# A two-layer graph convolution whose merges read 5 of 8 chunks, with the routing of finished nodes woven into the second layer's sums

## The reference

```python
xn = layernorm(x)                       # x: 3125 nodes x 256
# graph convolution, twice: 50000 edges (src, dst), sorted by dst, and a loop at every node
deg  = segment_sum(1, dst);  norm = rsqrt(deg)[src] * rsqrt(deg)[dst]
conv = lambda h, W, b: segment_sum((h @ W)[src] * norm, dst) + b
gnn  = conv(relu(conv(xn, W1, b1)), W2, b2)          # 256 -> 128 -> 256
# linear attention over all nodes (4 heads of 32, 4 memory slots), rmsnorm before and after
mix  = rmsnorm(attention(rmsnorm(xn)) @ w_out + b_out) + xn
x = x + gnn + mix
# mixture of experts: 8 experts, the best 2 of a token, hidden width 256
t = layernorm(x)
x = x + t + sum_e weight(t, e) * (gelu(t @ w1[e] + b1[e]) @ w2[e] + b2[e])
```

## Time and profile before

| | us |
|---|---|
| median of 3 runs | 755.34 |
| lowest and highest | 754.62, 762.78 |
| span of the profiled execution, first to last instruction | 754.8 |
| PE busy in it | 585.7 (78%) |
| DVE busy | 509.7 (68%) |
| ACT busy | 347.6 (46%) |
| POOL busy | 132.2 (18%) |

### The profile page before, as it was taken

The page is one execution under the profiler, slowest core; times in us unless marked ns, Lnnn a source line. Parts: engine busy times, 40 slices in busy tenths (PEclk is TensorE's granted clock), DMA queues, the critical chain, the costliest instruction groups (busy, mean ns, idle before and its releaser), DMA issues.

```text
span 754.8 us, 13942 instructions
## 1 busy us (share of the span) xinstructions
PE 585.7 (78%) x5198; PEld 516.7 (68%) x5198; DVE 509.7 (68%) x1114; ACT 347.6 (46%) x623; POOL 132.2 (18%) x133
## 2 busy tenths in 40 slices
PE   0889791879999999999599999989640499999500
PEld 0245351769999999987499999888530399999500
DVE  6773998459999999818556531299850577887534
ACT  0034773397777777710211111224240388999400
POOL 2000000000000000000000000018886145565600
PEclk9978996799999999999799999999755599999955
DMA  7999999301355531000056867503332245555198
GB/s 186 253 283 284 284 283 313 145 1 54 166 218 219 218 163 58 2 1 1 1 218 271 337 265 297 200 4 84 92 90 76 82 130 138 163 147 151 36 229 280
DMA packets 80158, 121.17 MB, mean 161 GB/s; under 512 B 8573, under 2 KB 68770, under 8 KB 78429
## 3 DMA queue, kind: packets, MB, share of 16 engines
q1 hardware_dynamic: 70621, 107.03, 46.8%
q0 software_dynamic: 9472, 13.27, 5.7%
HBM read 50.00 MB, written 72.21 MB: 162 GB/s over the span
## 4 chain that ended last, share of the span: by engine, by line
PE 48%; DVE 21%; DMA 9%; POOL 8%; issue 6%; ACT 5%; SPq 1%; DVEq 0%; ACTq 0%; POOLq 0%
PE psB L1216 21%; POOL expert_slots L571 8%; DVE hot L683 7%; PE psC L1122 3%; DMA back<-expert_out 3%; PE psC L1216 3%; PE psB L1369 3%; PE psA L1134 3%; DMA xs<-expert_slots 3%; PE psD L1134 2%; DMA acc<-in_x_dram 2%; PE psA L1357 2%; PE psC L1383 1%; ACT counts L1414 1%; PE psD L1383 1%
## 5 line engine op out<-in xcount | busy, mean ns | idle before, releaser
L1216 PE MATMUL psB<-hs,counts 125*128 125x256 f16 x1600 | 210.3, 275 | 3.3 <-DVE hs L790 2.7
L1216 PEld LDWEIGHTS psB<-hs,counts 125*128 125x128 f16 x1600 | 173.0, 140 | 4.9 <-issue 2.8
L683 DVE TENSOR_TENSOR hot<-iota_j,places 128x2048 bf16<-128x2048 bf16 x128 | 154.9, 1223 | 18.0 <-PE psA L1134 12.0
L563 POOL IOTA row_of<- 128x25 f32 x1 | 0.2, 238 | 475.3 <-PE psC L1216 475.3
L578 POOL DMA_INDIRECT expert_out<-y,to_row x64 | 65.8, 1029 | 62.3 <-DVE y L1060 49.4
L1414 ACT CAST counts<-psA 128x1000 f16<-128x1000 f32 x64 | 63.3, 989 | 15.2 <-PE psA L1134 15.2
L571 POOL DMA_INDIRECT expert_slots<-rows,place x50 | 62.1, 1241 | 45.2 <-issue 44.9
L1414 ACT CAST counts<-psD 128x1000 f16<-128x1000 f32 x64 | 63.6, 994 | 12.6 <-PE psD L1134 12.6
L1134 PE MATMUL psA<-hot 128*128 128x125 bf16 x512 | 49.4, 220 | 12.9 <-DVE hot L683 7.1
L1134 PEld LDWEIGHTS psA<-hot 128*128 128x128 bf16 x512 | 38.1, 98 | 22.8 <-DVE hot L683 12.4
L848 DVE TENSOR_TENSOR sum_both<-psB,sum_both 128x256 f32<-128x256 f32 x32 | 13.5, 422 | 57.7 <-ACT sum_both L1474 57.7
(11 more groups left out here) (286 smaller groups left out, 1067.0 us busy)
## 6 DMA issues: line engine op xcount, KB each, us to landing
expert_slots<-zeros SPq DMA_DIRECT2D x8, 3536.0 KB, 29.9
kept_counts<-counts SPq DMA_DIRECT2D x6, 4000.0 KB, 11.4
counts<-kept_counts SPq DMA_DIRECT2D x6, 4000.0 KB, 13.0
xs<-expert_slots SPq DMA_DIRECT2D x32, 272.0 KB, 3.1
back<-expert_out SPq DMA_DIRECT2D x5, 1120.0 KB
w_raw<-in_L_ffn_w_dram SPq DMA_DIRECT2D x2, 2048.0 KB, 11.5
acc<-in_x_dram SPq DMA_DIRECT2D x1, 2800.0 KB
out_dram<-acc SPq DMA_DIRECT2D x5, 560.0 KB
```

The lines of the kernel that those rows point to most:

```text
L683: v.tensor_tensor(hot[:, slot].rearrange("p g w n s -> p (g w) n s"), iota_j[:, :, :].unsqueeze(1).to_broadcast([P, 2 * pairs, P, PAIR]), ...
L1216: m = pe.matmul(sum_bank(g, d), counts5[0:PT, buf, a, d, :], hs2[0:PT, a, :, :].rearrange("p q f -> p (q f)"), start=a == 0 and first, sto ...
```

## The change

**Merges.** A window w of block c has steps between 125c + t and 125c + 124 + t, so a block's steps can lie in at most 5 chunks once all steps are moved up by 3 places (`AHEAD`): chunks 0 to 4, 1 to 5, 1 to 5, 2 to 6, 3 to 7 for blocks 0 to 4 (`chunks_of`). `merge` has 20 matmuls in place of 32, `merge_transposed` 2 + 10 for a node in place of 2 + 16.

**Layer 1** builds and sums chunks 7 down to 0. Before the sums of the eighth chunk in that order, blocks 4 and 3 are merged, in the middle of them blocks 2 and 1, after them block 0. The scale for layer 2 is now made in the beginning, together with that of layer 1, from a bound (the largest input plus the largest bias), so `spread_scale(1)`, the running maximum and its reductions are gone, and a block can be split into its halves as soon as it is there.

**Layer 2** sums chunks 1, 0, 2, 3, 4, 5, 6, 7; the first of them takes the blocks of features in the order 4 to 0. Block 0 is merged and routed inside chunk 5's sums, blocks 1 and 2 inside chunk 6's, block 3 inside chunk 7's and block 4 after them. The pieces of routing are written out by hand between fifths of a chunk (25 matmuls) on PE, and between the groups of sums on DVE and ACT.

**Memory.** `rows` and `tokT` get room of their own outside `counts`; `hs` and `sel` make place for `w1_now`, `xs`; the second weights `w2` lie in one tensor with the first (`w_split`); the outputs of `times_w2` move from psB and psC to psA and psD.

```diff
+FIRST_ORDER = [*range(CH - 1, -1, -1)]
+SECOND_ORDER = [1, 0, *range(BUFFERS, CH)]
+BLOCK_ORDER = [*range(C - 1, -1, -1)]
+AHEAD = 3
+def chunks_of(c):
+    first, last = AHEAD + PT * c, AHEAD + PT * c + PT - 1 + EDGE_TILES - 1
+    return [*range(first // P, last // P + 1)]
...
-                    for k in range(CH):
+                    for k in chunks_of(c):
                         for part in range(2):
...
-                    for k in range(CH):
...
-                    pe.wait_ge(sums_low_ok, SG * CH)
-                    for c in range(C):
-                        merge(c, max(c, 1), (psD, psA)[c % 2])
-                else:
-                    spread_scale(layer)
+            pe.wait_ge(counts_ok, UNITS * CH)
+            merge(0)
+            merge(1)
+            for i in range(2 * SLOTS):
+                add_sum((CH - 1) % BUFFERS, SUM_LIST, i, CH - 1)
+            merge(2)
+            merge(3)
+            for i in range(2 * SLOTS, len(SUM_LIST)):
+                add_sum((CH - 1) % BUFFERS, SUM_LIST, i, CH - 1)
+            merge(4)
...
-                        st.did(v.tensor_reduce(hs_max[0:PT, bass.ds(c + 1, 1)], hs[0:PT, bass.ds(W * c, W), :].rearrange("p d f -> p (d f)"),
-                                               AX.X, ALU.max))
-                    st.wait()
-                    make_scale(1)
...
-                if c >= 2:
-                    pe.wait_ge(token_full_ok, 3 * (c - 1))
+                    pe.wait_ge(token_full_ok, 3 * c)
...
+            second_sums(7, 0, Q)
+            ranks(1)
+            merge_transposed(3)
+            second_sums(7, Q, 2 * Q)
+            token_transposes(2)
+            second_sums(7, 2 * Q, 3 * Q)
+            logits(2)
+            times_w2(3)
+            second_sums(7, 3 * Q, 4 * Q)
+            ranks(2)
+            second_sums(7, 4 * Q, 5 * Q)
+            token_transposes(3)
+
+            merge_transposed(4)
+            logits(3)
+            times_w2(4)
+            ranks(3)
+            token_transposes(4)
+            logits(4)
+            ranks(4)
```

More of the change, by code:

```diff
@@ L965, in slot_places, with second_layer @@
                 v.tensor_copy(place[0:PT, :, W * c:W * c + W], place_f[0:PT]).then_inc(place_ok, 1)
-            st.wait()
-            for c in range(C):
+            def second_layer(c):
                 a = acc[0:PT, W * c:W * c + W, :]
-                tok = rows[0:PT, c]
                 if c == 0:
@@ new lines, in sums_done @@
+            def sums_done(i, g):
+                sums_add(CH + i, g)
+                sums_low(SECOND_ORDER[i], CH + i, g)
+            v.wait_ge(acc_scale_ok, 2)
+            for i in range(C):
+                sums_done(i, 0)
+                scale_mix(i)
+                sums_done(i, 1)
+                add_mix(i)
+                sums_done(i, 2)
+                add_b2(i)
+            v.wait_ge(acc_mixed, SLOTS)
+            v.wait_ge(consts, CONSTS + 1)
+            st.did(v.tensor_scalar(before[:], ident_row[:], ident_col[:], None, ALU.is_gt))
@@ new lines, in _ @@
+            sums_done(5, 0)
+            second_layer(0)
+            tokens(0)
+            sums_done(5, 1)
+            sums_done(5, 2)
+            add_tokens(0)
+            router(0)
+            sums_done(6, 0)
+            slot_places(0)
+            second_layer(1)
+            tokens(1)
+            sums_done(6, 1)
+            sums_done(6, 2)
+            add_tokens(1)
+            router(1)
+            second_layer(2)
+            slot_places(1)
+            tokens(2)
+            sums_done(7, 0)
@@ L997, in _ @@
+            add_tokens(2)
+            router(2)
+            second_layer(3)
+            sums_done(7, 1)
+            slot_places(2)
+            tokens(3)
+            sums_done(7, 2)
+            add_tokens(3)
+            router(3)
+            second_layer(4)
+            slot_places(3)
+            tokens(4)
+            add_tokens(4)
+            router(4)
+            slot_places(4)
             v.wait_ge(total_in, 1)
@@ L1206, in _, with add_sum @@
             SUM_LIST = [(g, a, d) for g, ds in enumerate(SUM_GROUPS) for a in range(SLOTS) for d in ds]
-            def add_sum(buf, i, nth):
-                g, a, d = SUM_LIST[i]
-                first, last = d == SUM_GROUPS[g][0], d == SUM_GROUPS[g][-1]
-                if a == 0 and first and nth:
+            BY_BLOCK = [(g, W * c + m, d) for c in BLOCK_ORDER for g, ds in enumerate(SUM_GROUPS) for m in range(W) for d in ds]
+            def add_sum(buf, order, i, nth):
+                g, a, d = order[i]
+                first, last = all(o[0] != g for o in order[:i]), all(o[0] != g for o in order[i + 1:])
+                if first and nth:
@@ L1218, in add_sum, with merge @@
-                if a == SLOTS - 1 and last:
+                              start=first, stop=last, skip_group_check=True)
+                if last:
                     m.then_inc(summed, 1)
-            def merge(c, used, ps=psD):
-                pe.wait_ge(merge_used, used)
+            def merge(n):
+                c, ps = BLOCK_ORDER[n], (psD, psA)[n % 2]
+                pe.wait_ge(merge_used, max(n, 1))
+                pe.wait_ge(sums_low_ok, SG * (FIRST_ORDER.index(chunks_of(c)[0]) + 1))
@@ L1260, in merge_transposed @@
-            def merge_transposed(c, nodes=range(W)):
-                if c and 0 in nodes:
+            for k in range(CH - 1):
+                pe.wait_ge(counts_ok, UNITS * (k + 1))
+                due = 0
+                for j in range(2 * UNITS):
+                    g = 2 * UNITS * (k + 1) + j
+                    build(g, j, j // 2 % 2, (psA, psD)[j // 2 % 2])
+                    while 2 * UNITS * due < (len(SUM_LIST) - 6) * (j + 1):
+                        add_sum(k % BUFFERS, SUM_LIST, due, k)
+                        due += 1
+                for i in range(due, len(SUM_LIST)):
+                    add_sum(k % BUFFERS, SUM_LIST, i, k)
@@ L1263, in merge_transposed @@
+            def merge_transposed(c):
+                pe.wait_ge(sums_low_ok, SG * (CH + SECOND_ORDER.index(chunks_of(c)[-1]) + 1))
+                if c:
                     pe.wait_ge(second_sums_ok, 2 * c)
-                for d in nodes:
+                for d in range(W):
                     o = psD[:, PT * d:PT * d + PT] if d < 4 else psD[:, 512:512 + PT]
+                    if d == 4 and c:
+                        pe.wait_ge(second_ok, W * (c - 1) + 1)
                     for part in range(2):
@@ new lines, in sums_high @@
+            def sums_high(chunk, nth, g):
+                if SG * nth + g >= 2:
+                    act.wait_ge(sums_low_ok, SG * nth + g - 1)
+                act.wait_ge(summed, SG * nth + g + 1)
+                act.copy(sum_place(nth, g).rearrange("p (d f) -> p d f", f=HID), sum_parts(g)[:, :, 1, :]).then_inc(sums_out, 1)
+                act.wait_ge(sums_added, SG * nth + g + 1)
+                act.activation(sum_part(0, chunk, g), sum_place(nth, g), ACT.Copy, scale=1.0 / P).then_inc(sums_high_ok, 1)
```

447 lines of the change are left out of this document (225 added, 222 removed).

## The result

| | before | changed |
|---|---|---|
| median, us | 755.78 (4 runs) | 717.8 (4 runs) |
| lowest and highest | 754.62, 762.78 | 716.98, 719.86 |
| span of the profiled execution | 754.8 | 718.0 |
| last scatter starts | 586.17 | 551.96 |
| first transposes of the experts | 594.29 | 559.79 |

The ratio is 0.9471, with a 95% interval of 0.9416 to 0.9526: 5.3% faster. (The two medians in the table give 0.9498, inside the interval.) Forecast were 715.0, with a range of 708 to 728. The profiled execution of the changed kernel is its longest of the four; the others have spans of 715.1 to 716.5.

A forecast was written before the change was run, and what follows sets the result against it. POOL's 79 us of scatters stood behind PE's 112 of sums, to be overlaid. From 754.8, less 41.5 for the last scatter's earlier start, plus 0.4 and 0.8, came 714.5; with 0.5 around the span 715.0, range 708 to 728.

The forecast's parts named there:

- small terms: Longer scale chain in the beginning, 0.4 us at most; handoffs between engines, 0.8; register operations in expert tiles, 0.
- End of layer 1: Five merges of 2.74 us instead of 4.39, placed among the sums; layer 2 starts at 350.4 without PE idling.
- the 17.4: Microseconds by which layer 2 was to start sooner, at 350.4 instead of 367.78.
- Layer 2 on PE: Eight chunks of 13.64 us plus 33.3 of merges and routing pieces; last sum ends at 492.8, no PE wait before.
- the late chain of 727: Rival: DVE's groups of sums in chunks 5 to 7 come late and PE waits, +12.6 us; chance 0.19.
- The chain of block 3: After the last sum: block 3's tokens, logits and router, slot numbers at 513.0, first scatter at 514.1.
- The scatters: Last 20 scatters on POOL run without pause at 1.61 us each; the last starts at 544.7, 41.5 us sooner.
- The page against it: Manual's rule that scatters contend with DVE's two-input SBUF additions: up to 1.2 us each, 2.4 in all, within the 1.61.
- The sign that I had named: On POOL: the prediction is wrong if the scatters' interval isn't 1.5 to 1.6 us.
- the rival of 722: Rival: the new `ISA` operations in the expert tiles show in the time, +7.7 us; chance 0.04.
- one fixed chain: Everything from the last scatter on stays as before: 8.12 us to the experts, then 160.5 to the end.
- Around the span: Time outside the execution's span: 0.5 us added to 714.5 for the forecast of 715.0.

The follow-up runs named there:

- experiment 1: Changed kernel with all routing put behind the sums of all eight chunks again, pieces still in the woven order; 757.61 us, ratio 0.9996.
- experiment 3: Kernel before, with only the merges of both layers cut to the five chunks holding a block's steps; 753.76 us, ratio 0.9951.
- experiment 4: Changed kernel with 40 idle matmuls on PE in its wait for block 3's tokens; 714.06 us, ratio 0.9424.
- experiment 6: Changed kernel with block 3's routing pieces moved forward on PE, DVE and ACT; 713.43 us, ratio 0.9418.
- experiment 7: Changed kernel with block 3's pieces moved forward on PE, DVE and ACT, plus 21 and 60 idle matmuls before tokens of blocks 3 and 4; 711.26 us, ratio 0.9394.

## Why the prediction was right

The mechanism was as put: PE ran through the woven stretch without a wait, with POOL's scatters beside it. That the time came so near is in part luck. The last scatter started at 551.96, 7.3 later than forecast, and what lies behind it was 3.8 shorter. Term by term, forecast span 714.5, measured 718.0:

| term | forecast | measured | off by |
|---|---|---|---|
| start of the first merge | 321.5 | 324.85 | +3.3 |
| first merge to layer 2 | 28.9 | 29.07 | +0.2 |
| layer 2's sums with all that is woven in | 142.4 | 141.9 | -0.5 |
| last sum to block 3's first scatter | 21.3 | 23.7 | +2.4 |
| 20 scatters | 30.6 | 32.5 | +1.9 |
| small terms | 1.2 | not seen apart from the others | -1.2 |
| last scatter to the experts' transposes | 8.12 | 7.83 | -0.3 |
| from there to the end | 160.5 | 158.2 | -2.3 |

**The start.** Ten of the other kernels shown here have the changed kernel's program before the first merge, but for edits in POOL, which is idle there, and that merge began between 320.93 (experiment 1) and 324.18; the changed kernel's profiled execution, at 324.85, is the latest of them. Eight of the ten give 320.93 to 322.07. So the 321.5 was right for most executions, and this one is a late one. Its window 120 to 168 has a granted clock of 0.74 and the kernel before 0.78 there, but executions with 0.75 had their first merge at 322, so the clock of that window doesn't explain it, and its cause stays open.

**End of layer 1.** Right in size and mechanism: PE waited 1.50 for `part2` (1.40 forecast), DVE made the features between merges, and no low clock was left in the first chunk. That the five chunks alone, 20 for 32 matmuls, were worth little I had not said; experiment 3 shows it. I had priced the 17.4 as one, and it came as one.

**Layer 2 on PE.** 8 x 13.64 + 33.3 came within 0.5 us, and no piece waited: the late chain of 727 did not happen.

**The chain of block 3.** The step that failed is that "`merge_transposed(4)` stands ahead of the logits, which run from 501.9 to 504.2": I gave block 4 "some 3 us later at half clock" and left block 3 at full clock, though I had PE wait there from 492.8 on for tokens at 497.5. With that wait filled the chain takes 21.1 (experiment 4).

**The scatters.** "I take 1.61: the odd long ones were spread over the 50" is mis-sized: they are not spread, each has a place. The 3.59 is tied to the 40th, and lies always in the last 20; of the long ones there is at most one to each of DVE's additions (below). 16 of the 19 intervals here are 1.49 or 1.50, the others 1.66 (a block's first scatter takes 1.35), 2.17 and 4.78, 32.5 in all. The sign that I had named, an interval of 1.5 to 1.6, holds for the usual one and not for the mean of these 19, 1.71.

**The page against it** held in kind. In all thirteen kernels every scatter of `expert_slots` of more than 1.65 us starts during one of DVE's five additions of two SBUF tensors, 1.49 us each. And how long is set by the addition: of the 51 scatters of all kernels that start during one, 48 end 1.06 to 1.07 us after its end; the other three start in its last 0.04 us and take the usual 1.19. So what a scatter loses is what is left of the addition when it starts, beyond 0.13 us, as if it could not go on beside it. In experiment 1, DVE and POOL:

```profile
517.09 1.49 DVE L975 TENSOR_TENSOR acc<-acc,rows 125x1280 f32<-125x1280 f32 x1
```

```profile
517.76 1.88 POOL L559 DMA_INDIRECT expert_slots<-rows,place  x1 [0.30 <-issue]
```

In the changed kernel it is 483.74 on DVE beside the 2.48 at 483.80, and 520.42 beside the 1.87 at 521.11. That is as the Trainium skill, GPSIMD Engine Reference, Specifications, would have it, which has the SBUF interfaces shared with VectorE. It costs up to 1.3 an addition and 0.7 in all of the last 30, where I had allowed 2.4: the one scatter that starts during the addition at 501.03 does so 0.03 us before its end. The other DVE work beside the changed kernel's scatters left them at 1.18 to 1.22.

**The fixed end.** The experts' transposes went from 559.8 to 667.4, 107.6, against 107.1 (594.3 to 701.4) before: the new `ISA` operations cost at most 0.5 over 32 tiles, which is less than the spread of this stretch (106.3 to 110.8 in the ten experiments built on the changed kernel), and the rival of 722 is out. The 2.3 us less come from reading the results back, in the chain of waits of the kernel before and of the changed one:

```profile
721.09 25.72 DMA back<-expert_out
```

```profile
687.18 22.95 DMA back<-expert_out
```

the same transfers, 2.8 apart; no cause was tried. It is a spread between executions and no gain of the change: the same read takes 22.95 to 28.36 in the thirteen kernels, and from the experts' first transposes to the end it is 157.6 to 165.1 in the changed kernel and the ten experiments built on it. I had called all behind the last scatter "one fixed chain"; it isn't.

**Around the span** lie 1.9 us, not 0.5: 719.86 for the profiled 718.0, and the kernel before, too, has 1.8 to 1.9 in every run beside the experiments. I had compared one execution's span with the median of others.

So the span is 3.5 over the forecast: 3.3 from a late execution and 4.3 from errors of mine (clock, 40th scatter), while 4.3 went the other way, 2.3 of them by the spread of the last part, which is luck. Against the median of 717.8 the forecast is 2.8 short.

## What to carry to other kernels

Shortening an operation that alternates with another engine's work (merge and features, 4.39 against 4.23) gains only down to that engine's pace; ask what it makes possible instead, here that finished blocks can go ahead. An order of pieces is made for what lies between them: the woven order was worth about 20 us with the sums in it, and cost about 20 without. When a chain runs over three engines, move the piece on all three, and where PE will wait, price the next pieces at the low clock too. And compare two kernels from a common point of the program to another: here starts differed by 4 us and the last read by 5 where the programs were the same.

## What the runs showed that I had not expected

A 3.6 us pause before the 40th indirect scatter after a block's first slot numbers, in thirteen kernels, which 32 earlier scatters, with waits or without, don't move. And PE came out of a wait of 4.37 us at half clock, its pieces long until 506.4, but out of one of 2.60 us in experiment 6 at full clock (transposes 1.07), and there the merge nodes took 1.25 from 502.1 on, though PE had not waited again for over 0.9 us. In experiment 7, with that wait filled but for 0.33 us, the same nodes took 1.25 from 503.85 on.
